# Wide constant products ahead of the first transposes, query products together, and a re-ordered middle in a graph layer on one core

## The reference

```python
h = jnp.maximum(_layernorm(x, axis=-1), 0.0)             # rows normalised, then relu
# --- the layer, on h ---
xn  = _batchnorm(h, norm1_g, norm1_b)                    # statistics over the 1250 nodes
agg = segment_sum(xn[src], dst, num_segments=N) / max(degree, 1)
conv_out = relu(agg @ W_conv + b_conv)
q, k, v = heads(h[:256], Wq), heads(h[:256], Wk), heads(h[:256], Wv)    # 8 heads of 64
def phi(t, is_query):
    t = t * 64 ** -0.25
    u = einsum('bhnd,md->bhnm', t, proj)                 # 256 random features
    diag = 0.5 * sum(t * t, -1)
    return exp(u - diag - max(u)) / sqrt(256) + 1e-6     # max per query row; over all keys for k
kv   = einsum('bhnm,bhnd->bhmd', phi(k), v)
attn = einsum('bhnm,bhmd->bhnd', phi(q), kv) / normaliser
out  = x + _batchnorm(conv_out + attn @ Wo + h, norm2_g, norm2_b)
```

## Time and profile before

| | us |
|---|---|
| median of 3 runs | 180.65 (180.29 to 180.94) |
| the profiled execution's own time | 180.8 |
| its span, first to last instruction | 178.8 |
| TensorE busy | 162.6 |
| VectorE busy | 136.9 |
| ScalarE busy | 90.6 |
| GpSimd busy | 7.6 |

### The profile page before, as it was taken

How to read it: one execution, slowest core, us unless ns; L and a number is a source line. 1 busy time by engine, 2 the same in 40 slices (tenths; PEclk the granted TensorE clock), 3 DMA queues, 4 the chain that set the end, 5 groups by cost and what they waited for, 6 DMA issues and landing times.

```text
span 178.8 us, 2873 instructions
## 1 busy us (share of the span) xinstructions
PE 162.6 (91%) x1060; PEld 106.7 (60%) x1061; DVE 136.9 (77%) x309; ACT 90.6 (51%) x164; POOL 7.6 (4%) x22
## 2 busy tenths in 40 slices
PE   0299999998999999999999999999999999999950
PEld 0288888653445464664777779585465484664840
DVE  2888659979685859699774885994999998596681
ACT  3437959567796639996643444324900313104050
POOL 5008200000000000000000000000000000000000
PEclk9999999999999999999999999999999999999998
DMA  5996970000070000000000000000096005040036
GB/s 180 370 307 213 315 236 4 0 0 0 6 252 0 0 4 0 0 0 2 4 0 4 0 0 4 0 0 7 9 312 251 0 4 143 2 133 14 0 101 187
DMA packets 11883, 13.69 MB, mean 77 GB/s; under 512 B 1458, under 2 KB 6748, under 8 KB 11868
## 3 DMA queue, kind: packets, MB, share of 16 engines
q1 hardware_dynamic: 10476, 12.13, 21.2%
q10 hardware_dynamic: 1072, 1.10, 1.8%
q0 software_dynamic: 320, 0.26, 0.6%
HBM read 10.92 MB, written 2.56 MB: 75 GB/s over the span
## 4 chain that ended last, share of the span: by engine, by line
PE 79%; DVE 11%; ACT 4%; DMA 2%; issue 2%; DVEq 0%; ACTq 0%
PE bank L959 23%; PE bank L695 19%; PE bank L625 10%; PE bank L719 4%; PE bank L709 4%; PE bank L738 4%; PE bank L637 3%; PE bank L617 3%; PE bank L683 2%; DMA xs<-in_x 2%; PE bank L672 2%; PE bank L986 2%; DVE wc L1122 1%; DVE mxk L1145 1%; DVE xs L1387 1%
## 5 line engine op out<-in xcount | busy, mean ns | idle before, releaser
L695 PE MATMUL bank<-wc,xs 128*128 128x512 f32 (+1 forms) x80 | 38.5, 608 | 0.2 <-DVE gl L1198 0.2
L959 PE MATMUL bank<-r,gl 128*128 128x512 f16 (+1 forms) x120 | 38.1, 338 | 0.0
L959 PE MATMUL bank<-r,gh 128*128 128x512 f16 (+1 forms) x120 | 38.1, 339 | 0.0
L1066 DVE TENSOR_TENSOR ohb<-iota,bcol 128x1280 f16<-128x1280 f16 x25 | 20.4, 818 | 3.8 <-PE bank L637 3.7
L385 ACT ACTIVATE r<-bank 128x500 f16<-128x500 f32 x25 | 18.6, 770 | 3.4 <-PE bank L637 3.4
L695 PEld LDWEIGHTS bank<-wc,xs 128*128 128x128 f32 (+1 forms) x80 | 13.6, 187 | 10.9 <-issue 10.9
L625 PE MATMUL bank<-hT,r 128*128 128x256 f32 x64 | 17.6, 439 | 0.0
L959 PEld LDWEIGHTS bank<-r,gh 128*128 128x128 f16 x120 | 11.6, 97 | 9.7 <-issue 0.3
L959 PEld LDWEIGHTS bank<-r,gl 128*128 128x128 f16 x120 | 11.7, 97 | 9.3
L595 ACT ACTIVATE bw<-mv,epst 128x1 f32<-128x1 f32 x4 | 1.2, 295 | 31.4 <-DVE mv L1363 31.4
L625 PEld LDWEIGHTS bank<-hT,r 128*128 128x128 f32 x64 | 14.0, 223 | 2.9 <-issue 0.4
(11 more groups left out here) (175 smaller groups left out, 263.5 us busy)
## 6 DMA issues: line engine op xcount, KB each, us to landing
xs<-in_x SPq DMA_DIRECT2D x15, 256.0 KB, 4.8
out<-xs SPq DMA_DIRECT2D x7, 256.0 KB
r<-in_L_gnn_Wq SPq DMA_DIRECT2D x1, 1024.0 KB, 7.5
r<-in_L_gnn_Wk SPq DMA_DIRECT2D x1, 1024.0 KB
wc<-in_L_gnn_W_conv SPq DMA_DIRECT2D x1, 1024.0 KB, 9.4
wvo<-in_L_gnn_Wv SPq DMA_DIRECT2D x1, 1024.0 KB, 12.0
wvo<-in_L_gnn_Wo SPq DMA_DIRECT2D x1, 1024.0 KB, 5.2
xs<-in_x ACTq DMA_DIRECT2D x3, 256.0 KB, 4.4
```

The lines of the kernel that those rows point to most:

```text
L695: last = nc.tensor.matmul(acc[0:n, :], xnT[:, f, i * P:i * P + n], wc[:, f, :], start=(f == 0), stop=(f == FT - 1))
L959: last = nc.tensor.matmul(acc[:, 0:cn], gg[0:n, s, f * P:(f + 1) * P], A16[0:n, s, c0:c0 + cn], start=(s == 0 and gg is gh), stop=(s == NT ...
L1066: last = V.tensor_tensor(oh[:, s0:s0 + n, :].rearrange("p s (m t) -> p s m t", t=2), iota16[:, 0:size].rearrange("p (m t) -> p m t", t=2). ...
```

## The change

1. Before anything else TensorE issues 18 products of the constant `cone` (float16, 128x128 stationary, 512 columns moving) into bank 0, which nothing reads, and three more between the edge search and the first query product.
2. Both query products come in front of the transposes of tiles 2 to 5. ScalarE copies only `q` 0, VectorE copies `q` 1, and ScalarE's squares of both stand behind the layer normalisation of tiles 6 to 9.
3. VectorE no longer adds the two halves of the comparison; the edge search sums 20 products of one column instead of 10. `first_rows` stands in front of the moments of tiles 2 to 5.
4. The edge values live in `qe` and no longer in `r2`.
5. GpSimd scales `W_conv`, behind its gathers; VectorE's four products are gone.
6. The lists of TensorE, ScalarE and VectorE in the middle are re-ordered, and `order` with them.

```diff
+ROUSE, ROUSE_MORE = 18, 3
...
-        g = r2[0:GROWS, 0:512].bitcast(I32).rearrange("p (q e) -> p q e", q=2)
+        ge = qe[:, :, :, :].rearrange("p q t m -> p (q t m)")
+        g = ge[0:GROWS, 0:512].bitcast(I32).rearrange("p (q e) -> p q e", q=2)
...
-        order = [("hT", 0), ("hT", 1), ("first",), ("q", 0), ("hT", 2), ("hT", 3), ("hT", 4), ("hT", 5), ("consts",),
+        order = [("hT", 0), ("hT", 1), ("first",), ("q", 0), ("q", 1), ("hT", 2), ("hT", 3), ("hT", 4), ("hT", 5),
...
(gpsimd, behind the gathers)
+            pool.wait_ge(crow_ready, 1)
+            for f in range(FT):
+                nc.gpsimd.tensor_tensor(wc[:, f, :], wc[:, f, :], crow[:, :], ALU.mult).then_inc(wc_scaled, 1)
...
(scalar: qk is split in qk_copy and squares)
-            qk(0, 0)
+            qk_copy(0, 0)
             store_hT(2)
...
             ln_tile(9)
-            qk(0, 1)
-            qk(1, 0)
+            squares(0, 0)
+            squares(0, 1)
+            qk_copy(1, 0)
+            squares(1, 0)
             store_hT(6)
...
             diag_copy(0)
-            edge_columns()
-            qk(1, 1)
+            qk_copy(1, 1)
             copy_uk(0)
             copy_uk(1)
+            edge_columns()
+            squares(1, 1)
+            copy_uk(2)
+            copy_uk(3)
             act.wait_ge(bn_var, 1)
             act.activation(bw[:, 1, :], mv1[:, :, 1], ACT.Sqrt, bias=epst[:, 0:1]).then_inc(bn_std, 1)
+            store_v(0)
+            copy_uk(4)
+            copy_uk(5)
             act.wait_ge(bn1_ready, 1)
             normal_xT(0)
...
(tensor)
+            def rouse(n):
+                for k in range(n):
+                    nc.tensor.matmul(bank[0][:, :], cone[:, :], cone[:, 0:1].to_broadcast([P, 512]), start=True, stop=True)
...
-                    for j in range(EJ // GR // 2):
+                    for j in range(EJ // GR):
...
+            rouse(ROUSE)
+            pe.wait_ge(id_set, 1)
             transpose_h(0)
             transpose_h(1)
             edge_search()
+            rouse(ROUSE_MORE)
...
             qk("q", wq, 0)
+            qk("q", wq, 1)
             transpose_h(2)
...
-            qk("q", wq, 1)
             pe.wait_ge(wk_in, 16)
             qk("k", wk, 0)
...
(vector)
+            def query_copy(i):
+                acc = landed(dve, "q", i)
+                V.tensor_scalar(qT[:, 2 * i:2 * i + 2, :], acc[:, :].rearrange("p (t n) -> p t n", t=2), QK_SCALE, None,
+                                ALU.mult).then_inc(read("q", i), 1)
...
-                V.tensor_tensor(below[:, 0:EJ // GR // 2, :], below[:, 0:EJ // GR // 2, :], below[:, EJ // GR // 2:, :], ALU.add
-                                ).then_inc(nb_ready, 1)
...
             edge_thresholds()
+            first_rows()
             ln_stats(1)
-            first_rows()
             ln_scale(1)
             ln_stats(2)
             ln_scale(2)
+            query_copy(1)
             bn_piece(0)
...
             diagonals(0)
-            for f in range(FT):
-                scale_weights(f)
             one_hots()
```

More of the change, by code:

```diff
@@ L403, in qk, with squares @@
                                ACT.Copy, scale=QK_SCALE).then_inc(read(nm, i), 1)
+            def squares(j, i):
+                nm, tT = (("q", qT), ("k", kT))[j]
                 stored(act, nm, i)
@@ L522, in _ @@
             store()
[L523 to L529, removed]
             high_part(0)
             diag_copy(1)
+            normal_xT(1)
             landed(act, "k", 1)
             q_feat(1)
+            high_part(1)
             q_exp(2)
@@ L779, in edge_search @@
                 for hf in range(2):
-                    for j in range(EJ // GR // 2):
+                    for j in range(EJ // GR):
                         last = nc.tensor.matmul(acc[0:GROWS, hf:hf + 1], below[:, j, hf * GROWS:(hf + 1) * GROWS],
-                                                cone[0:EP, 0:1], start=(j == 0), stop=(j == EJ // GR // 2 - 1))
+                                                cone[0:EP, 0:1], start=(j == 0), stop=(j == EJ // GR - 1))
                 last.then_inc(full("first"), 1)
@@ L854, in _ @@
             features("uk", kT, 0)
+            weight_sums()
+            columns()
             diag_T(0)
@@ L858, in _ @@
             values(0, 0)
+            values(0, 1)
+            stored(pe, "k", 1)
+            features("uk", kT, 2)
+            values(1, 0)
             count()
-            values(0, 1)
+            features("uk", kT, 3)
+            values(1, 1)
+            count()
             stored(pe, "q", 0)
@@ L863, in _ @@
             features("uq", qT, 0)
[L864 to L870, removed]
             project(0, 0)
             inverse_scales()
+            count()
             project(0, 1)
             diagonal(1)
+            project(1, 0)
             transpose_qf(0)
             transpose_qf(1)
-            project(1, 0)
+            project(1, 1)
             diag_T(1)
@@ L884, in _ @@
             project(2, 0)
-            count()
             transpose_qf(2)
             transpose_qf(3)
+            count()
             key_bias()
@@ L1223, in edge_thresholds @@
                 shape = [EP, EJ // GR, NW // 2, 2]
[L1224 to L1228, removed]
-                V.tensor_tensor(below[:, 0:EJ // GR // 2, :], below[:, 0:EJ // GR // 2, :], below[:, EJ // GR // 2:, :], ALU.add
-                                ).then_inc(nb_ready, 1)
+                V.tensor_tensor(below[:, :, :].rearrange("p j (w t) -> p j w t", t=2),
+                                edst2[:, :, :].unsqueeze(2).to_broadcast(shape),
+                                thr16[0:EP, :].rearrange("p (w t) -> p w t", t=2).unsqueeze(1).to_broadcast(shape),
+                                ALU.is_lt).then_inc(nb_ready, 1)
             dve.wait_ge(iota_set, 3)
@@ L1261, in _ @@
             key_max(3)
+            key_max(4)
+            key_max(5)
+            one_hots()
             q_bias(0)
@@ L1264, in _ @@
             one_hots()
[L1265 to L1268 removed]
             key_max(6)
             key_max_part(key_max(7))
+            inverse_scales()
             low_part(0)
             q_feat(0)
+            one_hots()
+            low_part(1)
             diagonals(1)
[L1274 removed]
             q_bias(2)
             q_bias(3)
+            one_hots()
             key_max_spread()
[L1278 to L1279 removed]
             key_biases()
```

36 lines of the change are left out of this document (11 added, 25 removed), and 6 rows, old and new, of the table order.

## The result

| | before | changed |
|---|---|---|
| median of the runs, us | 180.76 (180.29 to 180.94, 4 runs) | 178.05 (177.92 to 179.64, 4 runs) |
| ratio | | 0.9881, 95% interval [0.9845, 0.9918] |
| profiled execution, us | 180.8 | 178.1 |
| its span, us | 178.8 | 176.3 |

The change makes the kernel 1.2% faster by the ratio (0.8 to 1.6%); the medians lie 2.7 us apart. Forecast were 176.4 us and a lead of 4.2 us. The start came as the sum has it. What is missing was lost in the middle, by an edit that the sum had priced at nothing.

A forecast was written before the change was run, and what follows sets the result against it. It took TensorE, busy 162.6 of 178.8 us, to bound the kernel. Start 3.0, less 0.2 for key weights, plus 1.4 of stops gave 4.2 us off the profiled 180.8, so 176.4 by the median; range 175.2 to 178.8.

The forecast's parts named there:

- The start: Up to the query pair: wide products lift TensorE's clock early, the pair ends at 18.0 instead of 21.0, lead 3.0 us.
- the sum: Whole kernel: 3.0 for the start, less 0.2 for key weights, plus 1.4 of stops, 4.2 us off, giving 176.4.
- What bounds the kernel: Whole kernel: TensorE, busy 162.6 of 178.8 us; an earlier start reaches the end unless VectorE or ScalarE limits.
- rivals 2 and 4: Start: 2, clock rises only at 10.6, 178.1, chance 0.09; 4, clock not lifted or falls back, 183.2, chance 0.06.
- From 32.68 to 66.45: Middle stretch: re-ordered lists remove 1.4 us of TensorE's stops (bounds 0 and 2.3), bringing the lead to 4.2.
- W_conv's scaling: Middle: moving 2.50 us of VectorE's work to GpSimd, which has 10.2 us for it, counted as nothing.
- Rival 3: Middle: GpSimd is late, each scaling product above 2.55 us costing TensorE four times the excess; 178.2, chance 0.05.
- Rival 1: Middle: the stops only move, a bank read late stopping TensorE, key weights perhaps late; 177.7 to 178.8, chance 0.16.

The follow-up runs named there:

- gp_after_bn: Changed kernel, but GpSimd starts its four W_conv products only when VectorE has finished `bn_scale`: 176.23 us, ratio to before 0.9777.
- diag_first: Changed kernel, but VectorE's `diagonals(0)` stands ahead of `bn_scale`, GpSimd left as it is: 176.41 us, ratio to before 0.9777.
- scale_on_dve: Changed kernel, but VectorE scales W_conv again, behind `diagonals(0)`, and GpSimd only gathers: 176.29 us, ratio to before 0.977.
- before_plus_wide: Kernel before with only the 18 and 3 wide products added: 180.61 us, ratio to before 1.0019.
- no_wide: Changed kernel without any wide product of constants: 181.22 us, ratio to before 1.0057.
- gp_halves: Changed kernel with GpSimd's four products of 512 columns cut into eight of 256: 178.8 us, one execution.
- both: Changed kernel with GpSimd waiting for `bn1_ready` and `diagonals(0)` ahead of `bn_scale`: 176.12 us, ratio to before 0.9772.

## Why the prediction was right or wrong

**What bounds the kernel: right.** A lead that is there at the aggregation reaches the end. In `gp_after_bn` the aggregation starts 4.47 us earlier and the time falls by 4.3.

**The start: right.** Forecast: pair from 10.9 to 18.0, second key product ending near 29.9 with the key weights late by 0.2 (bounds 0 and 3.1). Measured: 10.77 to 17.84, and 29.59 with no wait for the weights. The search's twenty products cost 1.27 at the upper level (1.17 taken). Lead 3.07 for 2.8. The doubt about the clock (rivals 2 and 4) is answered: with eighteen wide products it rises near 4.6 us, an estimate, and the level holds; without them 3.2 us are lost by the medians.

**From 32.68 to 66.45: the re-ordering right, the term not collected.** 1.4 us of stops were to vanish. In the changed kernel one of 1.8 stands in their place. Where GpSimd's products no longer meet the small instructions they are gone: the first product with W_conv starts at 44.66 in `gp_after_bn` (forecast 45.4) and at 46.69 in the changed kernel.

**W_conv's scaling: here the prediction failed.** It said "I count it as nothing". The bounds were set for GpSimd's own product and for its deadline. Three of the four products took 1.26 us, inside the bounds of 0.52 to 1.6, and the first took 2.16, outside them; the deadline held, since GpSimd was done at 39.60, long before 45. The estimate that the forecast made from the Trainium skill (GPSIMD Engine Reference, Elementwise: side-by-side cycle accounting) was 1.1 us; the page's 4497 ns are for an add, which the forecast calls a product.

What had no price was what GpSimd's products do to VectorE. The forecast told from the Trainium skill (GPSIMD Engine Reference, Key points) that the memory port is shared while VectorE runs instructions with two inputs. The runs here agree, with 1.2 us for 0.16. But the forecast looked for such instructions only among the one-hots, and put their delay into no sum. In the changed kernel the one-hots ran in 0.80 and 0.40 us, the first of them having started ahead of GpSimd, and four small instructions of `bn_scale`, linked one behind the other, waited for one product each: 3.6 us. The bank of the diagonals was therefore read at 39.94 and not at 36.17 (`gp_after_bn`), and the value product of tile 1, which TensorE could have started at 38.34, started at 40.16. These 1.8 us stand in the sum as 0.

**The rivals.** Rival 3 named the shared port, and put the loss in the wrong place (TensorE waiting for GpSimd, or one-hots stretched); its figure, 178.2, is close to the 178.05 measured only because the 1.8 us that it took for another reason are by chance those of the stop. Rival 1 gave 177.7 to 178.8 and holds the time, and also the event: the old stops went, and a bank read late stopped TensorE, which an order with the reading in front avoids (`diag_first`). It didn't have the cause. The reasons that it gave were ScalarE's and VectorE's new order and late key weights; the weights were in time, and in the same order without GpSimd's products beside the chain (`gp_after_bn`, `scale_on_dve`) there is no stop. Its upper end is a small slip: 2.0 us off the median of the runs are 178.65, not 178.8.

**What was not asked.** The forecast added terms as if the clock's gain stood by itself. The wide products alone (`before_plus_wide`) gain nothing, and in the changed kernel they are worth 3.2 us. The traces give the likely reason: the query pair fills the time in which a faster TensorE would wait for tiles, and the later one-hot gives VectorE its slack; the two were not tried one by one. The rest of the change without wide products (`no_wide`) is 0.6% slower than before, but its trace still has a stop of 1.7 us for the diagonals' bank. Without both it wasn't tried, and so it is not shown that the rest needs the wide products.

## What to carry to other kernels

Before moving elementwise work to GpSimd, list the VectorE instructions with two inputs that will run beside it. Each GpSimd product with two inputs held up one of them here, however small that one was, for as long as the product had still to run, so the price can come near the total time of the GpSimd products (3.6 to 4.0 of 5.7 to 5.8 us). Then ask who waits for the last instruction of that chain. Put GpSimd's work beside other instructions (here the key maxima), or move the wanted instruction ahead of the chain. Waking TensorE early paid here only where the work behind it had its inputs by then, so look for an independent product to fill the gap, and check the engine that feeds the next stage.

## What the hardware showed that was not expected

- A VectorE instruction on 128x4 numbers with two inputs took 1.19 to 1.20 us beside GpSimd's two-input products of 1.26 us, 0.65 beside products of half the size (0.72), and 0.16 to 0.21 beside one-input products of 1.48.
- Whether the first float16 one-hot of a pair is slowed went by who started first. Where it started 0.1 us ahead of GpSimd it kept its 0.80 us and GpSimd's product took 2.16 (changed kernel); where GpSimd was 0.1 us ahead it took 1.86 (`no_wide`), or 1.31 beside products of half the size (`gp_halves`). The second one-hot of a pair whose first had started ahead of GpSimd waited in `gp_after_bn` and `both` (1.48 for 0.41) and not in the changed kernel (0.40); what decides there, the runs don't show.
- The column of the granted clock reads 1.00 while products of 512 columns take 0.43 us and while they take 0.22. Only the durations show the level.
